# A decoder kernel on one core: the second of two norms in a row takes its variance from the first

## The reference

```python
def _layernorm(x, axis=-1, eps=1e-05):
    m = jnp.mean(x, axis=axis, keepdims=True)
    v = jnp.var(x, axis=axis, keepdims=True)
    return (x - m) / jnp.sqrt(v + eps)
```

## Time and profile before

| | |
|---|---|
| median of 3 runs | 1718.77 us (1718.17 to 1722.68) |
| profiled execution | 1719.18 us |
| its span, first to last instruction | 1717.9 us |
| mean granted TensorE clock | 0.987 |
| PE (TensorE matmul) busy | 1602.5 us, 93% |
| PEld (weight load) busy | 819.7 us, 48% |
| DVE (VectorE) busy | 1035.5 us, 60% |
| ACT (ScalarE) busy | 902.8 us, 53% |
| POOL (GpSimd) busy | 431.4 us, 25% |

### The profile page before, as it was taken

One profiled execution on the slowest core, in us unless ns is written; L12 is line 12 of the kernel. 1 busy time (PEld: TensorE's weight loads), 2 busy tenths in 40 slices (PEclk: granted clock), 3 DMA queues, 4 the chain that ended last, 5 costly groups with the idle time before them and its releaser, 6 DMA issues.

```text
span 1717.9 us, 22306 instructions
## 1 busy us (share of the span) xinstructions
PE 1602.5 (93%) x7484; PEld 819.7 (48%) x7486; DVE 1035.5 (60%) x2138; ACT 902.8 (53%) x1740; POOL 431.4 (25%) x545
## 2 busy tenths in 40 slices
PE   7999999999999899999898999999898889999997
PEld 3344445344666344444333555555443435455545
DVE  5731116383313789999937788888448715565516
ACT  2531215253333577777836678787433744555513
POOL 1000100000000155555403565555210102233300
PEclk9999999999999999999998999999999999999999
DMA  6000100101000000000027221111127102000000
GB/s 236 0 1 0 43 0 1 37 0 74 1 1 19 1 19 10 10 19 1 29 99 247 90 79 42 29 29 29 62 58 234 49 10 94 12 23 12 1 0 25
DMA packets 36887, 74.11 MB, mean 43 GB/s; under 512 B 4459, under 2 KB 23403, under 8 KB 35339
## 3 DMA queue, kind: packets, MB, share of 16 engines
q1 hardware_dynamic: 36774, 72.68, 13.2%
HBM read 55.79 MB, written 16.78 MB: 42 GB/s over the span
## 4 chain that ended last, share of the span: by engine, by line
PE 61%; DVE 8%; ACT 4%; issue 4%; DMA 1%; SPq 1%; POOL 1%; DVEq 0%; PEldq 0%; POOLq 0%; ACTq 0%; PEld 0%
PE ps L2261 6%; PE ps L1843 3%; PE ps L1370 3%; PE ps L1396 3%; PE ps L3183 3%; PE ps L1819 3%; PE ps L1865 3%; PE ps L2250 3%; PE ps L3148 3%; PE ps L3158 3%; PE ps L3203 2%; PE ps L2272 2%; PE ps L1829 2%; PE ps L3178 2%; PE ps L3216 2%
## 5 line engine op out<-in xcount | busy, mean ns | idle before, releaser
L2515 POOL TENSOR_TENSOR work<-work,arena_b 128x512 f32<-128x512 f32 x128 | 167.3, 1309 | 125.6 <-ACT work L2377 125.6
L2467 DVE CUSTOM_DVE_ANT_0 work<-ps,arena_a 128x1024 f32<-128x1024 f32 x128 | 154.7, 1210 | 0.3 <-PE ps L2250 0.3
L2359 ACT ACTIVATE work<-work,small 128x1024 f32<-128x1024 f32 x128 | 146.6, 1145 | 4.6 <-DVE small L2467 4.6
L2261 PE MATMUL ps<-identity,work 128*128 128x128 f32 x1024 | 139.6, 278 | 8.8 <-ACT work L2377 4.7
L2261 PEld LDWEIGHTS ps<-identity,work 128*128 128x128 f32 x1024 | 115.7, 143 | 57.1 <-issue 29.6
L3367 POOL TENSOR_SCALAR ctx_keys<-ctx_keys,small 128x128 f32<-128x128 f32 (+3 forms) x128 | 67.2, 539 | 172.2 <-DVE small L3290 172.2
L2479 DVE TENSOR_TENSOR work<-ps,arena_b 128x512 f32<-128x512 f32 x128 | 87.9, 687 | 35.8 <-PE ps L2261 34.0
L2377 ACT ACTIVATE work<-ps 128x512 f32<-128x512 f32 x128 | 76.2, 595 | 61.4 <-PE ps L2261 60.2
L2250 PE MATMUL ps<-work 96*128 96x512 bf16 x256 | 79.7, 395 | 13.2 <-DVE small L2467 8.0
L2037 POOL TENSOR_SCALAR work<-work 128x1024 f32<-128x1024 int32 x64 | 66.7, 1042 | 100.6 <-DVE work L1990 100.2
L214 ACT ACTIVATE norm_parts<-normed 128x1024 f32<-128x1024 f32 x23 | 24.3, 1055 | 119.0 <-DVE normed L207 119.0
(11 more groups left out here) (407 smaller groups left out, 3319.2 us busy)
## 6 DMA issues: line engine op xcount, KB each, us to landing
work<-parts_k_L_xattn SPq DMA_DIRECT2D x14, 384.0 KB, 4.0
arena_a<-in_mask SPq DMA_DIRECT2D x2, 2048.0 KB, 7.6
arena_b<-in_groupT SPq DMA_DIRECT2D x2, 2048.0 KB, 9.5
head_weights<-in_w_L_xattn SPq DMA_DIRECT2D x8, 449.0 KB, 3.2
arena_a<-in_w_l_attn SPq DMA_DIRECT2D x1, 3072.0 KB, 14.2
head_weights<-in_w_L_attn SPq DMA_DIRECT2D x8, 384.0 KB, 3.1
work<-parts_q_L_attn SPq DMA_DIRECT2D x8, 384.0 KB, 4.6
work<-parts_k_L_attn SPq DMA_DIRECT2D x8, 384.0 KB, 5.3
```

Of the source, the lines that this page charges most:

```text
L2261: mm = pe.transpose(t_psum[z][:, kt * P:(kt + 1) * P], prob[i % NP][:, o:o + P], k.iden[:, :])
L2359: act.activation(p, p, ACT.Exp, scale=-1.0, bias=minmax[:, i % 8:i % 8 + 1], accum_out=sums[:, i % 8:i % 8 + 1]).then_inc(*exped.up())
L2467: dve.tensor_tensor_reduce(prob[i % NP], s_psum[i % NS], NEG[:, b, qt, :], -1.0, BIG * 3e8, OP.add, OP.min, minmax[:, i % 8:i % 8 + 1]).th ...
L2515: pool.tensor_tensor(p, p, GT[:, b, 4:8, qt * P:(qt + 1) * P], OP.mult).then_inc(*weighed_pool.up())
```

## The change

The outer norm centres, so the mean of what it gives is zero, and its variance is v / (v + eps), with v the variance that the first norm has computed. The change drops the mean, the centre, the square and the variance of the second norm and the object `ln2`. `variance_again` multiplies the variance in the PSUM bank twice by the first root; `root_again` takes Ln (with eps) and Exp on ScalarE; `norm_again` multiplies the normed value by the result into `r3`; `widen` applies weight and bias on ScalarE and writes `hpad`. The new scratch `again` lies where the shared square and root of the first norm were, and the first norm uses a square and a root for each half. On TensorE the two means and the two variances of the first norm follow one another, with 4 fillers before the first variance and 40 behind the second; on VectorE the convolution of half 0 is one piece ahead of the scale of half 1; GpSimd waits for `norm_again`.

```diff
--- before.py
+++ after.py
@@ -316,13 +316,14 @@
     if nxt:
         nxt.early, nxt.second = 2, True
     bank = lambda *i: [k.bank(j) for j in i]
-    ln2 = Norm(k, Hn, r3, bank(2, 3), sq, tmp, "L0_attn_ln1_w", "L0_attn_ln1_b",
-               put=[hpad[:, :, n, 3:] for n in range(B)], spare=k.bank(4))
+    ln1.sq, ln1.tmp, ln1.shared = sq, tmp, False
+    again = [k.tmp, k.sq[:, 0, :]]
     ln3 = Norm(k, ao, r3, bank(6, 7), sq, tmp, spare=k.bank(1))
     ln4 = Norm(k, r3, h2, bank(6, 7), sq, tmp, "L0_attn_ln2_w", "L0_attn_ln2_b", spare=k.bank(1))
     weights_in, cos_in, mlp_in = k.signals("dma", 3)
     qk, sumsq, v_, g_, o_, gated, upped, downed = k.signals("pe", 8)
-    k_out, k_sq, v_out, inverse, n_log, n_inv, g_out, o_out, silu = k.signals("act", 9)
+    k_out, k_sq, v_out, inverse, n_log, n_inv, g_out, o_out, silu, twice, widened = k.signals("act", 11)
+    ratio, spread = k.signals("dve", 2)
     tap, decay, floored, khat, state, kr_done, decayed, memory, x2_done, hidden, resid = k.signals("dve", 11)
     padded, scalars, shifted, x_early = k.signals("pool", 4)
     GATE, UP = (2, 3), (4, 5)
@@ -340,23 +341,19 @@
         return mm
 
     def tensor(pe):
-        ln1.begin_tensor(pe)
-        ln2.mean(pe, 0, ln1.out(1), beats=9)
+        ln1.mean(pe, 0)
         ln1.mean(pe, 1)
-        ln2.var(pe, 0, beats=12)
+        ln1.var(pe, 0, beats=4)
         ln1.var(pe, 1)
-        ln2.mean(pe, 1, ln1.out(2), beats=9)
+        k.beat(k.bank(4), 40)
         pe.wait_ge(*weights_in(1))
         pe.wait_ge(*cos_in(2))
-        k.beat(k.bank(4), 15)
-        ln2.var(pe, 1)
         pe.wait_ge(*tap(8))
         enter(pe, "qk", 4, 0).then_inc(*qk.up())
         project(pe, 6, W["v"], xc[0], 0)
         pe.wait_ge(*k_sq(1))
         magnitudes(pe, 0)
         project(pe, 7, W["v"], xc[0], 1).then_inc(*v_.up())
-        pe.wait_ge(*ln2.logged(2))
         enter(pe, "g", 2, 0).then_inc(*g_.up())
         pe.wait_ge(*k_out(1))
         pe.wait_ge(*tap(16))
@@ -440,17 +437,18 @@
 
     def scalar(act):
         act.preload_act_table_set(LN_EXP)
-        ln1.begin_scalar(act)
-        ln1.square(act, 1)
-        ln2.square(act, 0)
-        ln2.root(act, 0)
-        ln1.root(act, 1)
+        for n in range(B):
+            ln1.square(act, n)
+        for n in range(B):
+            ln1.root(act, n)
+        root_again(act, 0)
+        widen(act, 0)
         act.wait_ge(*decay(8))
         act.activation(rdec, rdec, ACT.Ln).then_inc(*inverse.up())
         act.wait_ge(*inverse(1))
         act.activation(rdec, rdec, ACT.Exp, scale=-1.0).then_inc(*inverse.up())
-        ln2.square(act, 1)
-        ln2.root(act, 1)
+        root_again(act, 1)
+        widen(act, 1)
         keys(act, 0)
         unit(act, 0)
         values(act, 0, 6)
@@ -482,6 +480,19 @@
             act.preload_act_table_set(LN_EXP)
             nxt.root(act, 0)
 
+    def root_again(act, b):
+
+        act.wait_ge(*ratio(2 * b + 2))
+        act.activation(again[b], again[b], ACT.Ln, bias=k.eps).then_inc(*twice.up())
+        act.wait_ge(*twice(2 * b + 1))
+        act.activation(again[b], again[b], ACT.Exp, scale=-0.5).then_inc(*twice.up())
+
+    def widen(act, b):
+        act.wait_ge(*spread(b + 1))
+        for c in range(DC):
+            act.activation(hpad[:, c, b, 3:], r3[b][:, c, :], ACT.Identity, scale=k.col("L0_attn_ln1_w", c),
+                           bias=k.col("L0_attn_ln1_b", c)).then_inc(*widened.up())
+
     def keys(act, b):
         ps = k.ps[:, 4 * S:6 * S].rearrange("p (c s) -> p c s", c=DC)
         act.wait_ge(*qk(b + 1))
@@ -529,22 +540,21 @@
             dve.wait_ge(*decay(3 + 3 * c))
             dve.tensor_tensor_scan(dec[:, c, 1:S], gam[:, 1:S], ones[:, 1:S], 1.0, OP.mult,
                                    OP.mult).then_inc(*decay.up())
-        ln1.begin_vector(dve)
-        ln1.centre(dve, 1)
-        ln2.centre(dve, 0)
+        for n in range(B):
+            ln1.centre(dve, n)
         dve.wait_ge(*decay(7))
         dve.tensor_scalar(rdec, dec, 1e-6, None, OP.add).then_inc(*decay.up())
-        ln2.scale(dve, 0)
+        variance_again(dve, 0)
+        ln1.scale(dve, 0)
+        norm_again(dve, 0)
+        variance_again(dve, 1)
+        dve.wait_ge(*padded(1))
+        dve.wait_ge(*widened(2))
+        for j in range(4):
+            convolve(dve, 0, j)
         ln1.scale(dve, 1)
-        dve.wait_ge(*padded(1))
-        dve.wait_ge(*ln2.out(1))
-        convolve(dve, 0, 0)
-        convolve(dve, 0, 1)
-        ln2.centre(dve, 1)
-        convolve(dve, 0, 2)
-        convolve(dve, 0, 3)
-        ln2.scale(dve, 1)
-        dve.wait_ge(*ln2.out(2))
+        norm_again(dve, 1)
+        dve.wait_ge(*widened(4))
         convolve(dve, 1, 0)
         convolve(dve, 1, 1)
         floor(dve, 0)
@@ -586,6 +596,19 @@
             nxt.scale(dve, 0)
         close(dve, 1)
 
+    def variance_again(dve, b):
+        dve.wait_ge(*ln1.rooted(b + 1))
+        dve.tensor_tensor(again[b], ln1.bank[b], tmp[b], OP.mult).then_inc(*ratio.up())
+        dve.wait_ge(*ratio(2 * b + 1))
+        dve.tensor_tensor(again[b], again[b], tmp[b], OP.mult).then_inc(*ratio.up())
+
+    def norm_again(dve, b):
+        dve.wait_ge(*ln1.out(b + 1))
+        dve.wait_ge(*twice(2 * b + 2))
+        for c in range(DC):
+            op = dve.tensor_tensor(r3[b][:, c, :], Hn[b][:, c, :], again[b], OP.mult)
+        op.then_inc(*spread.up())
+
     def convolve(dve, b, j):
         for c in range(DC):
             if j == 0:
@@ -671,7 +694,7 @@
                            OP.mult).then_inc(*scalars.up())
         pool.wait_ge(*scalars(2))
         for b in range(B):
-            pool.wait_ge(*ln2.centred(b + 1))
+            pool.wait_ge(*spread(b + 1))
             for c in range(DC):
                 pool.tensor_scalar(Hn[b][:, c, :], Hn[b][:, c, :], 1.0, bg[:, c:c + 1], OP.mult,
                                    OP.add).then_inc(*shifted.up())
```

## The result

The changed kernel takes 1707.72 us (median of 4 runs, 1704.75 to 1711.51) against 1718.47 for the one before: the ratio is 0.9935, with an interval of 0.9907 to 0.9963. That is 10.75 us faster, and the interval spans 6.4 to 16 us. In two later series it took 1709.02 (ratio 0.9941, 0.9927 to 0.9956) and 1709.23 (0.9931, 0.9914 to 0.9947). The profiled execution is the slowest of the four, 1711.51 us with a span of 1710.2 and a mean granted clock of 0.985.

What follows compares the result with a forecast made beforehand. A chain of norms and convolution over four engines sets the first projection's start, then TensorE bounds. Start from 39.54 to 28.8 gains 10.7 us: 1708.5 from the profiled 1719.18, 1708.1 from the median, stated 1708.3; range 1705.5 to 1712.5.

Steps and rivals of the forecast that it cites:

- What bounds the kernel: First block: a chain of norms and convolution sets the first projection's start; ending earlier by the same amount, 10.7 us.
- (c): Rival: behind the first projection a queue that does not move takes the gain back; 1715 to 1719 us, chance 0.04.
- (b): Rival: Identity in the widening needs another table, loads of 1.28 us each; 1711 us, chance 0.03.
- Up to the first root: Start of the first norm: fillers and slow TensorE delay half 0's first Exp from 16.8 to 17.4, costing 0.55 us.
- The second norm of half 0: Variance operations from 17.4, Ln and Exp 19.15 to 20.5, multiplication into r3 to 21.8, widening 1.45 us to 23.3.
- The convolution: Half 0's eight operations take 4.97 us plus 0.4 contention with GpSimd (bounds 0 and 0.79); last tap at 28.7.
- Behind the first projection: Later work keeps its distance: keys' square at 4.0 us, half 1's taps at 4.0, floor at 7.2; cost nothing to 0.3.
- the cover of 0.24 us for the keys: Behind the first projection: slack between the keys' weight load and its matmul, said to absorb ScalarE running 0.25 us too long.
- The clock: Rival: TensorE's clock falls after idling 2.7 us ahead of the first projection; costs 1.6 us, 1709.9, worst 1711.5; chance 0.22.

Runs made afterwards that it cites:

- e1_fill50: The changed kernel with 50 fillers behind the second variance in place of 40, ending just before the last tap; median 1708.21 us.
- e0_again: The changed kernel run once more with nothing altered, as the measure of the runs beside it; median 1709.02 us.
- e3_vector_wb: The changed kernel with weight and bias of the second norm back on VectorE; median 1709.60 us against 1709.02 for the changed kernel.
- e5_warm: The changed kernel with 50 fillers in place of 40, plus 12 matmuls on the constant matrix ahead of the input; median 1708.54 us.
- e10_changed: The changed kernel run once more with nothing altered, as the measure of two runs on the same chip; 1709.23 us.

## Why the prediction was right

The median came out 0.6 us below the 1708.3 that was forecast. That it is so near is luck: the interval of the gain spans some 10 us, and in two later series the changed kernel was 9.8 and 11.4 us faster. By the steps:

- **What bounds the kernel.** Right: the first projection moved, and all behind it moved with it; from it to the marker the distance is the same to 0.02 us when the clock holds (e1_fill50). No rival of a gain taken back later (c) showed, nor table loads (b): the two Identity activations are released by VectorE alone, and ScalarE loads no table between 8.0 and 41.07 us.
- **Up to the first root.** The profile shows no loss here where 0.55 was forecast: the first Exp ends at 16.66 and not at 17.4, and the centre of half 1 starts at 12.42, not 13.3. But e0_again has 13.59 and a first projection 1.0 later. The step took the moment at which TensorE's pace doubles from one trace and used it as a number. It differs from run to run, and since the second mean has taken the place of fillers, the chain now hangs on it. The forecast of 28.8 for the first projection lies in the band of 27.89 to 28.96 that the three profiles of the changed kernel show, near its upper end.
- **The second norm of half 0.** Right: from the first variance operation to the multiplication into r3 it is 19.75 - 16.69 = 3.06 us, forecast 3.15; ScalarE takes the second root right behind that of half 1, as said, and the widening takes 1.52 (forecast 1.45, bounds 1.27 and 1.56). From the multiplication into r3 to the first tap it is 2.96 us, forecast 2.80.
- **The convolution.** Contention was sized at 0.4 us. From the first tap to the projection it is 27.89 - 22.71 = 5.18 us, against 4.97 plus 0.05 for the handover and the 0.4. Beside GpSimd the variance operation took 0.80 us (0.69 alone) and the first pair of taps 0.98, start to start (0.91 before), 0.2 in all; the handover took 0.15. GpSimd's shift was over at 23.04 us, before the second pair. Added up against the forecast: the first root comes 0.7 us earlier, the second norm is 0.1 shorter, the way from the multiplication to the first tap 0.16 longer, and from there to the projection it is 0.27 shorter (5.18 for 5.45), which makes the 0.9.
- **Behind the first projection.** In e1_fill50, where the clock holds, the keys start 3.85 us behind the first projection (forecast 4.0), the first taps of half 1 at 3.98 (4.0) and the floor at 7.15 (7.18 before); the cover of 0.24 us for the keys was enough.
- **The clock.** The mechanism and its price of 1.6 us were right, the chance of 0.22 was too low. The fall came in each of the three profiles of the changed kernel and in e3_vector_wb, and in none with the wait filled. I had weighed one wait of 2.07 us without a fall against one of 2.36 with one as if they were even, although the forecast wait was the longest of the three. The trace of the kernel before had more to say. It has four waits of TensorE between 2.2 and 5 us behind its start (2.23, 2.33, 2.31 and 4.58 us; the second is the 2.36 of the earlier trace rows), and in or right behind each of the four the clock was at its lower level; of its five waits between 1.9 and 2.1 us that holds for one. The first of the four, and the stretch behind it:

```profile
292.12 1.42 PE L851 MATMUL ps<-identity,work 128*100 128x128 f32 x6 [2.23 <-DVE work L977]
```

```profile
292.45:295.86 3.41, 3.41 (x10) 1.97 (x9) 1.14 (x3) 1.93 (x6) 0.00 (x0) 0.54 0.00 0
```

The Trainium skill, page "TensorE: Matmul & The Clock Gate", section "Why this matters for your kernels", asks for no idle gap above some 3 us. That a gap below it keeps the clock is contradicted here: waits of 2.27 us, and of 1.96 us in e5_warm, were followed by the lower level.

So the total was right in part because two errors pull against each other in the profile: the chain was up to 0.9 us shorter than forecast, and the fall that I had left out of the sum took 1.6. A thing that the prediction did not do at all is to part the order from the shortcut. By the first projection nearly half of the gain is order (by the medians about a third), and would be had without the algebra.

## What to carry to other kernels

When a chain of small steps sets the start of a block, list what each engine is in when the chain reaches it; in this case running the two halves' norms side by side was worth 5.2 us and dropping the second statistics 6.2. Whenever a chain is shortened, count the fillers again: 40 left a wait of 2.3 us that gave 1.6 back, 50 did not. Where TensorE starts slow, a warm start pays only if the next engine is ready too; here it opened a new wait when alone, and with VectorE's early work beside it the two gave 1.9 to 3 us at the first projection.

## What the runs showed of the hardware that was not expected

- The clock fell after a wait of 1.96 us that had a shorter one before it (e5_warm), and after the wait of 2.26 to 2.27 us ahead of the first projection in every profile with one, at the price of 1.6 to 1.7 us. A wait of 10.89 us cost hardly more, 1.9, since the lower level ran in part while TensorE idled.
- The length of a wait does not decide it alone. The wait of 2.23 us at 292.12 us of the kernel before was followed by the lower level; the same wait in e10_changed (2.22 us, at 283.50) was not, its granted clock is 1.00 in it and for the 3.41 us behind it. Over the 13 profiles, 32 of the 43 waits of 2.2 to 2.4 us had the lower level within the 4 us behind them, and so had 25 of the 65 of 1.85 to 2.1 us. What else decides is open.
- The pace at the start varies between runs of one kernel: the 8 matmuls of the two means took 5.62 us in one profile of the changed kernel and 6.42 in another, and with 12 matmuls ahead of them 3.67.
- The spread of the runs of one kernel, some 9 us, goes with the mean granted clock of the run (0.990 to 0.985). The first block holds little of it: in the three profiles of the changed kernel its start varies by 1.1 us.
